# A graph layer with gated mixing and a feed-forward on selected rows: the FFN moved behind the loop, sparse sums on two banks, each tile's row chain one position later

## The chip, the cores and the metric

The kernel runs on one core of one Trainium2 chip. The metric is the device time of one execution in microseconds, median of the runs.

## The reference

`x` is (6250, 256) in float32, with 200,000 edges `src`, `dst`; `dst` is sorted and crowded at its low end.

```python
xn = layernorm(x)
# gnn
h_sparse = keep the 32 largest of each row of xn @ W_neigh
neigh = segment_sum(h_sparse[src], dst) / max(degree, 1)
gnn = xn @ W_self + neigh
# mix: softmax(k) over rows, per-head context, gate
mix = ((q @ (softmax(k, rows)^T v)) * sigmoid(gelu(ln(xn) @ Wg1 + bg1) @ Wg2 + bg2)) @ Wproj + bproj
x2 = x + gnn + mix
# ffn on the k - 1 = 3124 rows with the largest logit w, of 6250
x3 = layernorm(x2); w = x3 @ wr + br
y = (gelu(x3 @ w1 + b1) @ w2 + b2) * w          # w1 256x1024, w2 1024x256
out = x2 + x3 + (y where the row is selected, else 0)
```

## The kernel before, in words

Rows are taken in 50 tiles of T = 125. A first part (to about 407 us) normalises x, makes `h_sparse` as two float16 halves in `rows_d`, and prepares the context and the weights. Then comes the loop this case is about, three hardware loops in all (1, 3 and 1 turns of 10 positions), and behind it the selection.

A position n closes one tile's sum over edges. There are two kinds of tile. Eight **dense** tiles (the ones with most edges; n = 9, 14, 19, 24, 29, 34, 39, 46) are summed as a matrix of counts times all rows: `window` (DVE, L1458 and L1466) writes one-hots of pairs of edge chunks, `count_window` (PE, L1036) multiplies them into counts, ACT copies these out (L842), and `from_rows` (PE, L1107) multiplies the counts with rows that ACT's DMAs bring into `hs` in eight pieces (`load_h`, L515). This is spread over the positions ahead of the dense one (`SHARE`, `SUMMED`): 29 sparse positions have windows, 10 have pieces of `hs` instead, and the last three have neither. The 42 **sparse** tiles are summed by `visit`: POOL gathers 128 rows of 1 KB at a time by indirect DMA (L717), four to a group, into a ring of 8 groups; DVE writes the group's one-hots (L1439, a ring of 8); PE multiplies (L1062, and L1063 for the degree) and frees the slot. SP waits for the landings, tells PE, and refills the index stage.

Beside that each position has the work of its rows. PE: `ffn_down` (L1022) and `ffn_up` (L1014) of older rows, then `mix_hidden`, `project`, `mix_open` (L980 to L1006), all float32, then opens the sum's bank (bank 0 for every sparse tile, bank 1 for dense), turns x3, and visits. DVE: the one-hots, base sums (L1519, L1523), the two FFN rows operations (`ffn_rows`, L1429, L1431), then waits for PE's sum (`s_agg`, L1530), takes it out (L1531 to L1536), and runs the row chain (L1542 to L1573: x2, layer norm by an integer root, x3, logit). ACT: loads of x and of the turned rows, gate functions, the FFN's activation (L802), copies, the store of the FFN's rows. The FFN is computed for all rows of a tile, selected or not; its result goes to `yw_d`, x2 + x3 stays in SBUF (`res_all`).

Behind the loop DVE and PE search the threshold (ten rounds of seven candidates, L1606, L1164), with the FFN of the last three tiles between the rounds, compute a 0/1 mask, and DVE adds `mask * yw` into `res_all` (L1668), stored in ten parts by SP and ACT.

Positions are counted from 0; position n ends with the n-th L1530. A matmul in float32 shows as two records in the trace.

## Time and profile before

| | us |
|---|---|
| median of 3 runs | 2461.32 |
| lowest and highest run | 2454.12, 2475.36 |
| profiled execution, its span | 2470.0 |
| mean granted TensorE clock | 0.811 |

The span is from the first to the last instruction of one profiled execution; the times of the rows below are from its start. In a row of a timeline stand start, length, engine, line, operation, tiles and count, and in brackets the engine's idle time before it and what ended that. A row of a stretch has: from and to, length, then busy us and count for PE, PEld (weight loads), DVE, ACT and POOL, then the granted clock, the DMA engines' share and GB/s.

### The profile page before, as it was taken

The page shows a single profiled execution, that of the slowest core. Times are in us where ns is not written, and L with a number is a line of the kernel's source. Part 1 is how long each engine was busy: PE and PEld are TensorE (multiplying, and loading weights), DVE is VectorE, ACT ScalarE, POOL GpSimd, SP SyncE. Part 2 cuts the span into 40 slices and gives each one's busy share as a digit, 9 for nine tenths or more (in the row PEclk, how much of TensorE's full clock was granted, in tenths as well). Part 3 has the DMA queues.
Part 4 walks back from the last instruction along what each step waited for, and adds up shares of the span by engine and source line. Part 5 has one row for each costly group of instructions (what it writes and reads, how often), then busy time and mean ns, then how long its engine had stood idle before and what let it go on. Part 6 is the DMA issues. An engine that isn't in the chain of part 4 may idle for free. (4 is left out here: it accounts for less than half of the span.)

```text
span 2470.0 us, 40137 instructions
## 1 busy us (share of the span) xinstructions
PE 1713.3 (69%) x8913; PEld 1213.6 (49%) x8914; DVE 1289.5 (52%) x4086; ACT 456.7 (18%) x1009; POOL 1068.1 (43%) x1156
## 2 busy tenths in 40 slices
PE   1985556766556676667677767777767778776873
PEld 0552442444335454445455545545545656555662
DVE  6999536544344235635462653553454553644357
ACT  1542210111011011111121111211111212221220
POOL 1455634555544634553443454344244253444230
PEclk8997667777767877888788888878888888888886
DMA  8221422222223522262236227227127127226337
GB/s 168 68 77 55 124 61 64 71 75 79 85 75 103 153 74 65 76 167 75 66 101 138 59 75 178 57 70 184 50 67 186 49 72 165 68 72 149 90 77 188
DMA packets 173360, 239.30 MB, mean 97 GB/s; under 512 B 34148, under 2 KB 141950, under 8 KB 173214
## 3 DMA queue, kind: packets, MB, share of 16 engines
q0 software_dynamic: 46336, 126.03, 18.7%
q10 hardware_dynamic: 87262, 82.20, 13.1%
q1 hardware_dynamic: 39615, 29.27, 5.1%
q8 instruction: 74, 1.21, 0.2%
q14 instruction: 73, 0.59, 0.1%
HBM read 210.89 MB, written 26.01 MB: 96 GB/s over the span
## 5 line engine op out<-in xcount | busy, mean ns | idle before, releaser
L717 POOL DMA_INDIRECT ring<-rows_d,stage x960 | 948.4, 988 | 1174.9 <-PE bank L1062 812.0
L1062 PE MATMUL bank<-ring,region_v 128*125 x1120 | 399.5, 463 | 115.5 <-issue 108.3
L1036 PE MATMUL bank<-region_k 128*125 x830 | 291.6, 456 | 184.1 <-issue 164.7
L1530 DVE TENSOR_SCALAR col_deg<-bank 125x1 f32<-125x1 f32 x50 | 7.9, 158 | 610.9 <-remote 321.9
L1466 DVE TENSOR_SCALAR region_k<-iota,win_start,region_k 128x500 f16 x830 | 305.1, 407 | 29.7 <-issue 26.4
L1439 DVE SCALAR_TENSOR_TENSOR region_v<-iota,tile_start,dstT 128x500 f16 x280 | 205.6, 739 | 182.7 <-issue 144.4
L1062 PEld LDWEIGHTS bank<-ring,region_v 128*125 x1120 | 171.5, 153 | 246.0 <-issue 185.7
L1022 PE MATMUL bank<-region_v 128*125 128x256 f32 x848 | 243.5, 440 | 68.6 <-issue 68.3
L1014 PE MATMUL bank<-region_v 128*128 128x125 f32 x1664 | 230.8, 295 | 73.4 <-issue 72.8
L1036 PEld LDWEIGHTS bank<-region_k 128*125 x830 | 114.6, 151 | 312.0 <-issue 299.7
L1014 PEld LDWEIGHTS bank<-region_v 128*128 128x128 f32 x1664 | 222.9, 210 | 87.9 <-issue 84.6
L1458 DVE SCALAR_TENSOR_TENSOR region_k<-iota,region_k 128x250 f16 x415 | 173.4, 418 | 168.6 <-issue 130.4
L1022 PEld LDWEIGHTS bank<-region_v 128*125 128x125 f32 x848 | 181.8, 221 | 108.0 <-issue 78.8
L842 ACT ACTIVATE region_k<-bank 125x500 f16<-125x500 f32 (+1 forms) x104 | 60.2, 579 | 927.5 <-remote 483.9
L1063 PE MATMUL bank<-ones,region_v 128*125 128x2 f16 x1120 | 197.0, 176 | 3.4 <-issue 3.4
L1063 PEld LDWEIGHTS bank<-ones,region_v 128*125 x1120 | 176.8, 158 | 6.4 <-issue 4.1
L1107 PE MATMUL bank<-region_k 125*125 125x512 f16 x400 | 114.2, 427 | 71.7 <-DMA region_k<-rows_d 65.1
L802 ACT ACTIVATE region_v<-bank,b 128x125 f32<-128x125 f32 x416 | 112.2, 381 | 86.3 <-PE bank L1014 61.8
L789 ACT ACT_TABLE_LOAD x51 | 65.4, 1283 | 261.6 <-issue 119.3
L1107 PEld LDWEIGHTS bank<-region_k 125*125 125x125 f16 x400 | 56.0, 152 | 107.9 <-DMA region_k<-rows_d 72.4
L802 ACT ACT_TABLE_LOAD x51 | 65.4, 1283 | 183.3 <-PE bank L1022 87.7
L925 PE MATMUL bank<-region_r 128*125 128x512 f32 x200 | 96.6, 606 | 0.0
(283 smaller groups left out, 1958.1 us busy)
## 6 DMA issues: line engine op xcount, KB each, us to landing
region_k<-rows_d ACTq DMA_DIRECT2D x48, 672.0 KB
ring<-rows_d,stage POOLq DMA_INDIRECT x960
region_k<-rows_d ACTq DMA_DIRECT2D x16, 784.0 KB
region_v<-xT_d ACTq DMA_DIRECT2D x53, 125.0 KB
xT_d<-region_r ACTq DMA_DIRECT2D x51, 125.0 KB, 2.1
rows_d<-region_r SPq DMA_DIRECT2D x50, 125.0 KB
region_k<-in_x_dram ACTq DMA_DIRECT2D x50, 125.0 KB
yw_d<-region_v ACTq DMA_DIRECT2D x50, 125.0 KB
```

The source lines that it names most:

```text
L717: pool.indirect_dma_start(out=ring[:, c, :], out_offset=None, in_=rows_d, in_offset=bass.IndirectOffsetOnAxis(ap=stage[:, c:c + 1], axis=0 ...
L802: last = act.activation(hidT[:, n, :], bank[(7, 4)[n // 4]][:, n % 4 * T:(n % 4 + 1) * T], ACT.Gelu_apprx_tanh, bias=b1[:, n:n + 1])
L925: m = pe.matmul(bank[1 + s % 2][0:T, :], xT[:, s % 2, k * T:(k + 1) * T], wkv[:, k, :], start=(k == 0), stop=(k == KC - 1))
L1014: m = pe.matmul(bank[(7, 4)[n // 4]][:, n % 4 * T:(n % 4 + 1) * T], w1[:, k, n * 128:(n + 1) * 128], x3T[:, k, :], start=(k == 0), stop=(k ...
L1022: m = pe.matmul(out, hidT[:, n, :], w2[:, n, :], start=(n == 0), stop=(n == NH - 1), skip_group_check=True)
L1036: m = pe.matmul(out, lo, key, start=False, stop=False, skip_group_check=True)
L1062: m = pe.matmul(total, onehot_s, row_s, start=False, stop=False, skip_group_check=True)
L1063: d = pe.matmul(deg_sum, onehot_s, ones16[:], start=False, stop=False, skip_group_check=True)
L1107: m = pe.matmul(dense_sum, counts16[:, b, :], hs[:, q % 2, (b - first) * 2 * C:(b - first + 1) * 2 * C], start=False, stop=False, skip_gro ...
L1439: dve.scalar_tensor_tensor(out=part(hot_bytes, HOT, SLOT_HOT, hot, 0, SLOT_HOT).bitcast(F16).rearrange("p (a t) -> p a t", a=GC), in0=iota ...
L1458: dve.scalar_tensor_tensor(out=part(pair_bytes, HOT_PAIRS, SLOT_PAIR, slot, 0, KEYS_AT).bitcast(F16) .rearrange("p (a t) -> p a t", a=PAIR ...
L1466: last = dve.tensor_scalar(part(pair_bytes, HOT_PAIRS, SLOT_PAIR, slot, KEYS_AT + u * KEYS * 2, KEYS * 2).bitcast(F16), iota[:, 0:KEYS], p ...
```

## The change

The FFN leaves the loop. Each position now writes x3, x2 + x3 and the logit of its tile to `kept_d` (516 words a row) and x2 + x3 to the output. Behind the loop the rank of every row is computed beside the mask; ranks are turned by one-hots and matmuls into `slots`, the row number of each of 3124 selected rows, 25 tiles of them (`SEL`); POOL gathers these rows from `kept_d`, PE and ACT run the FFN in seven teams of up to four tiles (matmuls 500 columns wide), DVE finishes, and POOL scatters the rows over the output. Sparse sums alternate between banks 0 and 4, and the row chain of a tile runs in the next position, behind that one's one-hots. Names of several semaphores in the first part are merged.

```diff
-        deg_sum = bank[2][0:T, 504:506]
+        deg_sum = bank[7][0:T, 0:2]
         def agg_bank(at):
-            return dense_sum if at.dense else bank[0][0:T, :]
+            return dense_sum if at.dense else bank[(0, 4)[at.s % 2]][0:T, :]
...
@@ gpsimd, behind the gathers
+            pool.wait_ge(s_slots, 1)
+            for g, team in enumerate(TEAMS):
+                for j in team:
+                    pool.indirect_dma_start(
+                        out=row_of(j), out_offset=None, in_=kept_d,
+                        in_offset=bass.IndirectOffsetOnAxis(ap=slots[:, j:j + 1], axis=0)).then_inc(s_kept[g], 16)
+            for j in range(SEL):
+                held = min(T, KEEP - j * T)
+                pool.wait_ge(s_fin, j + 1)
+                pool.indirect_dma_start(
+                    out=out_d, out_offset=bass.IndirectOffsetOnAxis(ap=slots[0:held, j:j + 1], axis=0),
+                    in_=row_of(j)[0:held, C:2 * C], in_offset=None).then_inc(s_out, 16)
@@ scalar
+            def store_row(at):
+                u = at.s % 2
+                act.wait_ge(s_res, at.n + 1)
+                act.dma_start(kept_t[:, bass.ds(at.tile, 1), :], rowbuf[:, u:u + 1, :]).then_inc(s_rowout[u], 16)
+                act.dma_start(out_t[:, bass.ds(at.tile, 1), :], rowbuf[:, u:u + 1, C:2 * C]).then_inc(s_rowout[u], 16)
             def position(at):
...
-                hidden(one)
-                keep_x3T(one)
+                act.wait_ge(s_m3, two)
                 gate_open(n + 1)
...
                 gate_hidden(n + 2)
-                act.wait_ge(s_yw, one)
-                act.dma_start(yw_t[:, bass.ds(n, 1), :], yw[:, s % 2:s % 2 + 1, :]).then_inc(s_ywout[s % 2], 16)
+                before = at.before()
+                if before is not None:
+                    store_row(before)
@@ tensor, position
-                pe.wait_ge(s_yw, here)
                 pe.wait_ge(s_pfree, here)
-                ffn_down(one, y_sum)
                 ends.look_ahead(at_)
-                ffn_up(one)
                 spans.look(at_)
-                pe.wait_ge(s_deg, here)
...
-                pe.wait_ge(s_aggfree, here)
+                last = at_.before()
+                pe.wait_ge(s_aggfree, one if last is None or last.dense else here)
+                pe.wait_ge(s_deg, here)
@@ tensor, behind the loop
+            for t in range(NT):
+                pe.wait_ge(s_hotA, t + 1)
+                m = pe.matmul(bank[3][0:T, 0:2 * SEL], rank_hot[:, t, :], tile_ids[:, t, :], start=(t == 0), stop=(t == NT - 1))
+            m.then_inc(s_ids, 1)
...
+            pe.wait_ge(s_slots, 1)
+            turn_x3(0)
+            ffn_up(0, 0, NH - 2)
+            turn_x3(1)
+            ffn_up(0, NH - 2, NH)
+            for g in range(1, len(TEAMS)):
+                ffn_up(g)
+                if g + 1 < len(TEAMS):
+                    turn_x3(g + 1)
+                ffn_down(g - 1)
+            ffn_down(len(TEAMS) - 1)
@@ vector, position
                 if not at_.dense:
                     gathered()
                 ...
+                before = at_.before()
+                if before is not None:
+                    row_chain(before)
                 ...
                 dve.tensor_tensor(base_p, base_x, p_sum, ALU.add).then_inc(s_pfree, 1)
-                hold(dve, s_ywout[u], (half + 1) * 16)
-                ffn_rows(st, n, y_sum, yw[:, u, :], one)
+                gate_pre(n + 2, u, half + 1, two)
+                mix(two)
                 ...
                 dve.wait_ge(s_agg, one)
                 dve.tensor_scalar(col["deg"][:], deg_sum[:, 0:1], 1.0, None, ALU.max).then_inc(s_deg, 1)
                 ...
                 dve.scalar_tensor_tensor(out=agg_sum, in0=total[:, C:2 * C], scalar=1.0 / LO_SCALE,
                                          in1=junk, op0=ALU.mult, op1=ALU.add).then_inc(s_aggfree, 1)
-                gate_pre(n + 2, u, half + 1, two)
-                mix(two)
-                a = st.mark(dve.scalar_tensor_tensor(out=x2, in0=agg_sum, scalar=col["rdeg"][:, 0:1], in1=base_p,
@@ vector, behind the loop
+            dve.scalar_tensor_tensor(out=tile_hot, in0=iota[0:T, 0:SEL]...to_broadcast([T, NT, SEL]),
+                                     scalar=1000.0, in1=rough...to_broadcast([T, NT, SEL]), op0=ALU.add, op1=ALU.is_equal)
             for t in range(NT):
-                dve.scalar_tensor_tensor(out=res_all[:, t, :], in0=yw_all[:, t, :], scalar=selm[:, t:t + 1],
-                                         in1=res_all[:, t, :], op0=ALU.mult, op1=ALU.add).then_inc(s_fin, 1)
+                dve.tensor_scalar(rank_hot[:, t, :], iota[0:T, 0:T], rank_in[:, t:t + 1], None, ALU.is_equal).then_inc(s_hotA, 1)
...
```

In DVE's position the row chain (now the function `row_chain`) stood behind the sum of the halves and stands now behind the one-hots, for the tile before. The new helpers: `turn_x3(g)` turns a team's x3 tiles (two transposes each), `ffn_up(g)` makes 8 x 2 matmuls of up to 500 columns over four banks that ACT empties with the activation, and `ffn_down(g)` makes 8 matmuls of 256 columns for each tile of the team.

## Rows read from the trace of the kernel before

**Rows 1.** The page, part 1: busy us, share of the span, instructions.
```profile
PE 1713.3 (69%) x8913; PEld 1213.6 (49%) x8914; DVE 1289.5 (52%) x4086; ACT 456.7 (18%) x1009; POOL 1068.1 (43%) x1156
```

**Rows 2.** Groups by line, whole span: busy us, mean ns, idle before by releaser.
```profile
L717 POOL DMA_INDIRECT ring<-rows_d,stage x960 | 948.4, 988 | 1174.9 <-PE bank L1062 812.0 <-issue 267.9 <-remote 91.3
L1062 PE MATMUL bank<-ring,region_v 128*125 x1120 | 399.5, 463 | 115.5 <-issue 108.3 <-DVE region_v L1439 4.8 <-SPq L589 1.1
L1466 DVE TENSOR_SCALAR region_k<-iota,win_start,region_k 128x500 f16 x830 | 305.1, 407 | 29.7 <-issue 26.4 <-remote 2.2 <-PE bank L1036 0.8
L1036 PE MATMUL bank<-region_k 128*125 x830 | 291.6, 456 | 184.1 <-issue 164.7 <-DVE region_k L1466 14.5
...
L1530 DVE TENSOR_SCALAR col_deg<-bank 125x1 f32<-125x1 f32 x50 | 7.9, 158 | 610.9 <-remote 321.9 <-PE bank L1146 158.9 <-issue 130.0
```

**Rows 3.** Stretches of time: busy us of each engine, clock, DMA share, GB/s.
```profile
437.00:2397.00 1960.00, 1416.53 (x7692) 1023.45 (x7692) 925.11 (x2794) 341.96 (x739) 862.72 (x876) 0.82 0.37 96
...
622.00:681.00 59.00, 34.92 (x155) 23.03 (x155) 24.38 (x73) 5.08 (x13) 33.26 (x32) 0.70 0.28 81
...
884.00:901.00 17.00, 17.00 (x126) 14.68 (x125) 7.45 (x30) 7.06 (x14) 3.79 (x4) 0.80 0.38 102
...
1281.00:1324.00 43.00, 32.12 (x170) 22.38 (x169) 12.70 (x38) 7.01 (x15) 21.03 (x22) 0.84 0.90 203
...
1592.00:1637.00 45.00, 31.23 (x162) 22.29 (x161) 24.95 (x74) 8.14 (x17) 20.17 (x21) 0.81 0.26 74
...
692.70:697.00 4.30, 4.04 (x25) 2.33 (x25) 4.30 (x14) 0.00 (x0) 3.39 (x4) 1.00 0.25 69
...
697.00:711.60 14.60, 3.41 (x9) 1.31 (x9) 3.43 (x7) 0.00 (x0) 10.99 (x12) 0.66 0.36 106
```

**Rows 4.** Timeline of POOL in position 5: start, length, idle before.
```profile
692.68 0.95 POOL L717 DMA_INDIRECT ring<-rows_d,stage  x1 [15.71 <-PE bank L1062]
...
711.64 0.95 POOL L717 DMA_INDIRECT ring<-rows_d,stage  x1 [0.30 <-issue]
716.45 0.94 POOL L717 DMA_INDIRECT ring<-rows_d,stage  x1 [3.86 <-PE bank L1062]
```

**Rows 5.** Timeline of DVE in position 4.
```profile
622.45 0.16 DVE L1530 TENSOR_SCALAR col_deg<-bank 125x1 f32<-125x1 f32 x1 [14.29 <-remote]
...
623.88 0.48 DVE L1542 SCALAR_TENSOR_TENSOR region_v<-region_k,col_rdeg 125x256 f32<-125x256 f32 x1
...
630.96 2.39 DVE L1439 SCALAR_TENSOR_TENSOR region_v<-iota,tile_start,dstT 128x500 f16 x3 [1.00 <-DVE w_at L1573]
...
648.15 0.42 DVE L1519 TENSOR_TENSOR region_k<-region_k,region_v 125x256 f32<-125x256 f32 x1
...
649.50 0.35 DVE L1431 TENSOR_SCALAR region_v<-region_v,w_at 125x256 f32<-125x256 f32 x1
681.38 0.16 DVE L1530 TENSOR_SCALAR col_deg<-bank 125x1 f32<-125x1 f32 x1 [31.53 <-remote]
```

**Rows 6.** Timeline of PE: position 4, then the end of the loop and the search.
```profile
632.76 0.89 PE L980 MATMUL bank<-region_v,wg1g 128*64 128x125 f32 x4
...
636.30 0.61 PE L992 MATMUL bank<-hgT,wg 65*128 65x125 f32 x4
...
637.08 0.38 PE L1062 MATMUL bank<-ring,region_v 128*125 x1
...
2397.01 3.70 PE L1022 MATMUL bank<-region_v 128*125 128x256 f32 x16
2400.55 3.73 PE L1014 MATMUL bank<-region_v 128*128 128x125 f32 x32
...
2430.70 2.90 PE L1022 MATMUL bank<-region_v 128*125 128x256 f32 x6
```

**Rows 7.** Timeline of DVE behind the loop.
```profile
2404.21 0.20 DVE L1586 TENSOR_SCALAR_CACHE_REDUCE region_v<-w_all 125x50 f32<-125x50 f32 x1 [0.25 <-DVE w_at L1573]
...
2444.19 19.88 DVE L1668 SCALAR_TENSOR_TENSOR region_r<-region_k,region_v,region_r 125x256 f32<-125x256 f32 x50
```

More of the change, by code:

```diff
@@ L70, in build @@
     BODY = 10
-    assert NT * T == N and NT % BODY == 0 and C == 256
+    SEL = -(-KEEP // T)
+    WIDE = 4
+    RW = 2 * C + 4
+    TEAMS = [range(j, min(j + WIDE, SEL)) for j in range(0, SEL, WIDE)]
+    assert NT * T == N and (SEL - 1) * T < KEEP < SEL * T and NT % BODY == 0 and C == 256
     CHUNK = 128
@@ L220, in build @@
         hit_n = region_v.take([T, 7, NT])
[L221 to L222 removed]
+        masks = region_v.take([T, 2 * NT])
         selm = region_v.take([T, NT])
[L224 to L225 removed]
+        colcum = region_v.take([T, 2 * NT])
+        prefix = region_v.take([T, 2 * NT])
+        rank, rough, rank_tile, rank_in = (region_v.take([T, NT]) for _ in range(4))
+        slots = region_v.take([T, SEL], I32)
         after_search, region_v.at = region_v.at, at
@@ new lines, in ffn_up @@
+            def ffn_up(g, first=0, end=NH):
+                wide = len(TEAMS[g]) * T
+                pe.wait_ge(s_x3T, g + 1)
+                for n in range(first, end):
+                    if g * NH + n >= 4:
+                        pe.wait_ge(s_hid, g * NH + n - 3)
+                    for k in range(KC):
+                        m = pe.matmul(up_bank(n)[:, 0:wide], w1[:, k, n * 128:(n + 1) * 128], x3T[:, g % 2, k, 0:wide],
+                                      start=(k == 0), stop=(k == KC - 1))
+                    m.then_inc(s_up, 1)
@@ new lines, in _, with keep_x3T @@
+            dve.wait_ge(s_ids, 1)
+            a = st.mark(dve.tensor_copy(rank, bank[3][0:T, 0:NT]))
+            st.after(a)
+            dve.scalar_tensor_tensor(out=slots, in0=rank[:, SEL:2 * SEL], scalar=float(T), in1=rank[:, 0:SEL],
+                                     op0=ALU.mult, op1=ALU.add).then_inc(s_slots, 1)
+            def keep_x3T(g):
+                dve.wait_ge(s_tx3, g + 1)
+                wide = len(TEAMS[g]) * T
+                for k in range(KC):
+                    last = dve.tensor_copy(x3T[:, g % 2, k, 0:wide], bank[k][:, 0:wide])
+                last.then_inc(s_x3T, 1)
```

446 lines of the change are left out of this document (233 added, 213 removed).

## The prediction

> **What bounds the kernel now.** I read the page first, then the groups by line, then stretches of time, then the timelines of single positions, and last the end. The page [rows 1] shows no engine near its limit: PE 69 percent, DVE 52, POOL 43. So the kernel is bound by turns of engines. The reader should see in [rows 2] what the turns are: POOL's 960 gathers stand idle 1174.9 us, most of it (812.0) until a visit of PE frees a ring slot, and DVE stands idle 610.9 us (12 us in each of 50 positions) before L1530, until PE has closed a tile's sum. The loop from the first L1530 at 437 to the last at 2397 takes 1960 us [rows 3]. The profiled execution has a span of 2470.0 us and the median of the runs is 2461.3, 9 us less; I sum against 2470 and take 9 off at the end.
>
> One position shows the turns. Position 4 lies between the L1530 at 622.45 and that at 681.38, 58.9 us [rows 5]. PE's first visit starts at 637.08, 14.6 us in [rows 6]: until then PE does the FFN of an older tile and the mix, and DVE the chain of the last row (622.45 to 630.96). The ring is full, POOL waits: in position 5 it has waited 15.71 us when it starts again [rows 4]. From then on it issues 16 gathers in 692.68 to 711.64, one per 1.26 us, so a group of four takes 5.1 us. The reader should then compare two stretches of [rows 3]: in the first 4.3 us of these gathers PE is busy 4.04 and DVE 4.30; in the next 14.6 us PE is busy 3.41 and DVE 3.43, each 0.23 of the time, while POOL runs on. No data is missing there; I take it that long runs of gathers slow whatever PE and DVE issue, until POOL pauses (712.6 to 716.45 [rows 4]). I call these slowed stretches. What causes them the rows don't say. They tie a position to POOL's 32 gathers: 14.6 us without POOL, then about 40 us of gathers, then a few us to close.
>
> **What the change removes and adds in the loop.** (1) PE's FFN of a position goes: 16 records of L1022 in 3.70 us and 32 of L1014 in 3.73 us, 7.4 us at the full clock [rows 6]. What is left ahead of the first visit is the mix, 632.76 to 636.9, 4.1 us [rows 6]. DVE loses the two rows operations, some 0.8 us, ACT the eight activations. (2) The row chain (L1542 to the logits, 623.88 to about 629.95, 6.1 us [rows 5]) now stands behind the next tile's one-hots. So they start after the evacuation (622.45 to 623.5) and a us of loop bookkeeping, the 1.00 idle in [rows 5]: about 2 us after the sum is closed where it is 8.5 now. The two banks let PE start its visits without waiting for that evacuation, except behind a dense tile; the degree's column still has one place, and its wait is over within 0.2 us. (3) The waits that are added: ACT waits for the next mix (done early, it was queued ahead of the visits already) and for the row chain ahead of the two stores; behind it on ACT's queue stands the load of the next x tile, which DVE wants only a whole set of one-hots later. I cost both at nothing; without that cover each would show as a landing of a few us.
>
> DVE's own serial work barely shrinks. For position 4: evacuation 1.0, bookkeeping 1.0, one-hots 17.2 (630.96 to 648.15), chain 6.1, base sums and gate 1.3 (648.15 to 649.50 holds about this much besides the rows operations), mix 0.4 and look-ups 0.4: 27.4 us. PE's is mix 4.1, eight visits at 1.43 (399.5 us over 280) and twelve window pairs at 0.70 (291.6 over 415) [rows 2], at most 24, since slowed ones are in these means. With 32 gathers [rows 3] POOL needs 40 us. If nothing slowed anything the position would take 40 us; if DVE made no headway at all in slowed stretches it would take 27.4 + 33 = 60. DVE's headway there is bounded by 0.23 (one-hots, whose loops have many small steps [rows 3]) and 1; the chain is 21 short instructions without loops, so I take 0.3 for the mixture. Slowed time is 40 less 1.5 starts of 4.5 us, 33: DVE does 10 us there, and the position takes 17.4 + 33 = 50.4, a gain of 8. The stretch 1592 to 1637 [rows 3] holds a later, smaller position of 45.2 us with 20 or 21 gathers: DVE 27.1, slowed 18, DVE does 5.4 in it, so 21.7 + 18 = 39.7, a gain of 5.5. I take 6.5 for the 29 positions that have windows: 190 us.
>
> The ten sparse positions that sum rows from hs or lie beside that: 1281 to 1324 shows position 18, with the DMA share at 0.90 and 203 GB/s [rows 3]. They are bound by transfers, and the change adds some: 258 KB of kept rows and 128 KB of output instead of 125 KB, 0.26 MB or 1.3 us at that rate. PE's lost 7.4 us can help only where the DMAs are not the limit. I take 3 each, between -1.3 and 7.4: 30 us. The eight dense positions take 17.0 us with PE busy all of it [rows 3]; without 7.4 of PE, and DVE's 11 us as the next limit, I take 5 each: 40. The last three: 5 each, 15. The loop gains 190 + 30 + 40 + 15 = 275 us.
>
> **What it adds behind the loop.** Now 72.8 us pass from the last L1530 to the end. After: chain as now, 7.0 (2397.2 to 2404.21). The search up to the selected mask takes 40.0 (2404.21 to 2444.19 [rows 7]); it loses three pairs of rows operations, 2.4, and about 1.0 where PE's FFN parts held a round: 36.6. Ranks: six more DVE operations at 0.25, 1.5; the one-hot of 1250 elements, 1.8 (L1466 has 500 in 0.407 [rows 2], this form is slower). 50 rank one-hots of 125 columns: between 0.08 and 0.41 each, nearest to a quarter of the 500-column row plus its start, 0.18: 9 us, range 4 to 20. Last product, copy and slots 1.2. Four gathers of kept rows and their landing 6.5 (four at 1.26 plus something like 1.5; range 5 to 9). Turn and copy of the first team 3.2. The FFN: a record of 256 columns takes 0.231 (3.70 over 16), one of 125 columns 0.117 (3.73 over 32) [rows 6], so 0.44 for 500. A full team has 32 records up, 14.1 us, and 64 down, 14.8: 28.9 us, and there are 6.25 teams: 181. Turning the other tiles adds 50 pairs of 0.117: 11, of which 2 were counted. So 190. ACT's and DVE's part of it is half of what it was in all and lies beside PE. Behind the last product: sum, scaling, one scatter and its landing, 4. The sum is 7.0 + 36.6 + 1.5 + 1.8 + 9 + 1.2 + 6.5 + 3.2 + 190 + 4 = 261 us, 188 more than the 72.8 now. The fifty final sums (19.88 us [rows 7]) and the last stores are in these 72.8 and go. Setup is unchanged but for a missing 125 KB load.
>
> 2470 - 275 + 188 - 9 = 2374; I say 2375.
>
> **A rule against the change.** The gathers at 692.68 and after stand 1.26 us apart whether DVE is busy (until 697) or nearly idle [rows 3, 4]. The Trainium skill, "DMA: Bandwidth & Descriptors", section SWDGE vs HWDGE vs iDMA, says that GpSimd writes the descriptors of its DMAs into SBUF, and that certain VectorE operations lock it out of that while they run. By that rule DVE's busy time and POOL's would add up, and this change puts more DVE work beside gathers. So far the trace disagrees with it as a large cost; as a rival it is priced below from rows.
>
> **Rivals.**
> A. The turns dissolve: visits start about 5 us after the last sum instead of 14.6 and POOL's run starts as much earlier, and DVE's chain vanishes in time that it now idles (12 us a position [rows 2]). Then 42 sparse positions gain 9.6 each, 403, and the dense 40: 443, so 2470 - 443 + 188 - 9 = 2206. Its far end is POOL never waiting: 960 x 1.26 + 8 x 12 = 1306 for the loop, a gain of 654, 1995 in all. For it: 812 us of POOL's waiting. Against: the slowed stretches and the 203 GB/s of position 18.
> B. DVE becomes the serial bound in the loop. Its 27.4 us stay, its chain moves from a time in which POOL stands still into slowed stretches, and headway there is 0.1. Position 4 then takes 24.1 + 33 = 57.1, a gain of 1.8, the 29 windowed ones 52, the dense 40, the others nothing: 92. The end costs its 188: 2470 - 92 + 188 - 9 = 2557, slower. It decides as soon as the loop gains less than 188, 3.8 us a position. For it: DVE's sum is hardly smaller and PE's crawl at 0.23. Against: DVE's 610.9 us of idle time.
> C. The FFN behind the loop runs at the lower clock (1.2 instead of 2.4 GHz). After the gaps of the search six records of 256 columns take 2.90 us [rows 6], 0.48 each against 0.231. That would add 190: 2565. For it: PE's granted clock is 0.66 to 1.00 in the stretches of [rows 3]. Against: this FFN leaves PE hardly a gap, and 48 records in a row run at the full rate.
> D. The lock-out above: POOL's 862.7 and DVE's 925.1 us of the loop [rows 3], with the 0.30 us between gathers, would not overlap; 1210 + 925 = 2135, 175 more than now, so 2470 + 175 + 188 - 9 = 2824. [rows 4] beside [rows 3] speak against it: at 4.30 of 4.30 us of DVE POOL kept 1.26 us.
> That the change doesn't do what it says is covered by B: the banks alternate, but the freed wait was not the last one.
>
> **How the numbers follow.** Chances: forecast 0.51, A 0.26, B 0.16, C 0.05, D 0.01, rest 0.01. The forecast's own range is 2290 to 2460 (loop gain 190 to 350, end 175 to 215). For 8 in 10 I reach down past A's 2206 to 2140 and up to 2545, just short of B. One per cent, about what a measurement of this kernel tells from no change, is 2437 and 2486. Faster by more: nearly all of A and 0.42 of the forecast, 0.68. Within: 0.08 of the forecast and 0.04 of B and between, 0.12. Slower: 0.20.
>
> **What would show it.** The distance between two L1530-like waits in the windowed positions should fall from 58.9 to about 50 early and from 45 to about 40 later; below 45 and 36 it is A, above 56 and 43 B. The idle time before the first one-hots of a tile should be about a us, and DVE's idle time before closing a sum well under 600 us in all. POOL's wait for PE should fall by about what the loop gains. The end should be 250 to 275 us from the last sum, 28 to 30 us a team. The prediction is wrong if a team takes over 40 us, if POOL's gathers stand more than 1.4 us apart, or if position 18 takes under 30 us.

## The result, and the profile after

The changed kernel takes 2509.45 us in the median of four runs (2499.61 to 2514.48), the kernel before 2466.43 us in four runs beside them (2454.12 to 2475.36). The ratio is 1.0207, 95 percent interval 1.0131 to 1.0283; the two medians lie 43 us apart, 1.7 percent. The change is slower beyond the interval, where 2375 us and faster was forecast; whether by more than 2 percent is open. The runs below were made in five groups, each beside the kernel before, which took 1949, 1951 and 1952 us in three of the groups and 2460 and 2496 us (this last one run) in the other two, with the same code and data; I call these the quick and the slow condition, and the recorded result and the trace that the prediction rests on belong to the slow one. Gains and losses are compared within one condition.

The page of the changed kernel, its span and part 1 (busy us, share, instructions), against [rows 1]:
```profile
span 2497.5 us, 35631 instructions
PE 1546.7 (62%) x7023; PEld 1006.7 (40%) x7024; DVE 1280.0 (51%) x4041; ACT 238.0 (10%) x499; POOL 1129.9 (45%) x1207
```
Its groups by line, against [rows 2] (L729 is the old L717, L1616 the old L1530, L1606 the old L1519, L1015 the first matmul of the mix, old L980):
```profile
L729 POOL DMA_INDIRECT ring<-rows_d,stage x960 | 948.1, 988 | 1018.6 <-PE bank L1074 661.9 <-issue 265.5 <-remote 87.6
...
L1032 PE MATMUL bank<-region_v 128*125 128x256 f32 x200 | 93.0, 609 | 5.6 <-issue 5.6
...
L1015 PE MATMUL bank<-region_v,wg1g 128*64 128x125 f32 x208 | 51.9, 395 | 282.2 <-issue 262.3 <-DVE region_v L1471 8.6 <-remote 8.4
...
L1606 DVE TENSOR_TENSOR region_k<-region_k,region_v 125x256 f32<-125x256 f32 x50 | 21.3, 426 | 50.9 <-DMA region_k<-in_x_dram 32.2 <-issue 11.6 <-DVE region_v L1570 7.1
...
L1616 DVE TENSOR_SCALAR col_deg<-bank 125x1 f32<-125x1 f32 x50 | 7.8, 157 | 469.7 <-remote 216.7 <-issue 135.2 <-PE bank L1153 117.6
```
DVE's wait for the closing of a sum fell from 610.9 to 469.7 us and POOL's wait for PE from 812.0 to 661.9. But a new one stands ahead of the mix: 282.2 us of PE idle, nearly all "issue", where the same line of the kernel before has only 38.4 us. The records of the mix also got longer, as L1032 shows beside the same line of before, L997:
```profile
L997 PE MATMUL bank<-region_v 128*125 128x256 f32 x200 | 64.2, 449 | 0.0
...
L980 PE MATMUL bank<-region_v,wg1g 128*64 128x125 f32 x208 | 37.0, 305 | 38.4 <-issue 37.5 <-DVE region_v L1423 0.9
```
And the stretches, against [rows 3]: the loop from the first to the last closing of a sum, then the FFN behind it:
```profile
432.00:2236.00 1804.00, 1090.87 (x5242) 712.42 (x5242) 896.89 (x2696) 95.88 (x200) 862.51 (x876) 0.72 0.43 111
...
2311.40:2489.60 178.20, 178.07 (x666) 120.32 (x666) 25.70 (x49) 35.45 (x56) 46.69 (x40) 0.98 0.16 43
```
The loop takes 1804 us where it took 1960: a gain of 156, not of 275. The end takes 261.5 us from the last closing, against 72.8. The table sorts the loop by kind of position, from one closing to the next; the late stores are explained below.

| us, slow condition | before | change | forecast gain | gain | change with late stores | gain |
|---|---|---|---|---|---|---|
| windowed (28 of the 29; the first ends where the sum starts) | 1352 | 1259 | 183 | 93 | 1193 | 159 |
| with rows from hs (10) | 398 | 381 | 30 | 16 | 399 | -2 |
| dense (8) | 142 | 117 | 40 | 25 | 89 | 53 |
| last three | 68 | 46 | 15 | 22 | 54 | 14 |
| end, from the last closing | 72.8 | 261.5 | -188 | -188.7 | 260.2 | -187.4 |

Each column comes from one profiled execution. A second one of the kernel before has 1337, 407, 148 and 67 us in the first four rows, so gains of 10 us in a row say little. The profiled run with late stores was also the fastest of its ten, 19 us under their median: for all that stands ahead of the last closing, the medians of the runs give the change a gain of 146 us and the late stores one of 206, where the profiles give 161 and 237.

### The profile page after: what moved, and what is told of

Same layout as the page of the kernel before. It is cut to its first block, busy times and chain, and to the rows that moved or that the text cites. A ratio compares the mean times of both kernels' runs of the same rounds, so it can differ in the third digit from the quotient of the medians.

```text
span 2497.5 us, 35631 instructions
## 1 busy us (share of the span) xinstructions
PE 1546.7 (62%) x7023; PEld 1006.7 (40%) x7024; DVE 1280.0 (51%) x4041; ACT 238.0 (10%) x499; POOL 1129.9 (45%) x1207
## 4 chain that ended last, share of the span: by engine, by line
PE 29%; issue 26%; DVE 15%; DVEq 9%; another core or an unknown queue 9%; DMA 8%; ACTq 2%; SPq 1%; POOL 0%; ACT 0%; POOLq 0%
PE bank L1074 6%; PE bank L1048 6%; DMA region_k<-rows_d 5%; PE bank L1193 3%; PE bank L1207 3%; DVE region_k L1507 2%; PE bank L1117 2%; DVEq L459 2%; PE bank L1032 2%; DVEq L1518 2%; DMA gs_wide<-gs_d 2%; DVE region_r L1381 1%; PE bank L1035 1%; DMA region_k<-in_x_dram 1%
## 5 line engine op out<-in xcount | busy, mean ns | idle before, releaser
L729 POOL DMA_INDIRECT ring<-rows_d,stage x960 | 948.1, 988 | 1018.6 <-PE bank L1074 661.9
L1074 PE MATMUL bank<-ring,region_v 128*125 x1120 | 418.9, 478 | 119.1 <-issue 113.9
L1074 PEld LDWEIGHTS bank<-ring,region_v 128*125 x1120 | 178.1, 159 | 250.7 <-issue 195.8
L1616 DVE TENSOR_SCALAR col_deg<-bank 125x1 f32<-125x1 f32 x50 | 7.8, 157 | 469.7 <-remote 216.7
L1015 PE MATMUL bank<-region_v,wg1g 128*64 128x125 f32 x208 | 51.9, 395 | 282.2 <-issue 262.3
L1075 PEld LDWEIGHTS bank<-ones,region_v 128*125 x1120 | 182.5, 163 | 18.7 <-issue 16.9
L1117 PE MATMUL bank<-region_k 125*125 125x512 f16 x400 | 127.8, 467 | 90.9 <-DMA region_k<-rows_d 76.4
L1015 PEld LDWEIGHTS bank<-region_v,wg1g 128*64 128x64 f32 x208 | 33.7, 201 | 286.4 <-issue 283.1
L1032 PE MATMUL bank<-region_v 128*125 128x256 f32 x200 | 93.0, 609 | 5.6 <-issue 5.6
L1193 PE MATMUL bank<-region_k,region_v 128*128 128x500 f32 (+1 forms) x224 | 88.2, 553 | 1.4 <-DVE region_k L1733 1.4
L1207 PE MATMUL bank<-region_v,region_k 128*125 128x256 f32 x400 | 87.3, 379 | 0.0
L753 POOL DMA_INDIRECT out_dram<-region_r,region_v x24 | 28.6, 1191 | 126.8 <-DVE region_r L1753 123.1
L1035 PE MATMUL bank<-region_v 128*125 128x256 f32 x200 | 79.6, 535 | 7.9 <-issue 7.9
```

The source lines that it names most:

```text
L729: pool.indirect_dma_start(out=ring[:, c, :], out_offset=None, in_=rows_d, in_offset=bass.IndirectOffsetOnAxis(ap=stage[:, c:c + 1], axis=0 ...
L1032: pe.matmul(p_sum, xTc[:, turn, k * T:(k + 1) * T], w_self[:, k, :], start=(k == 0), stop=False)
L1035: m = pe.matmul(p_sum, mixT[:, k, :], wproj[:, k, :], start=False, stop=(k == KC - 1))
L1074: m = pe.matmul(total, onehot_s, row_s, start=False, stop=False, skip_group_check=True)
L1075: d = pe.matmul(deg_sum, onehot_s, ones16[:], start=False, stop=False, skip_group_check=True)
L1117: m = pe.matmul(dense_sum, counts16[:, b, :], hs[:, q % 2, (b - first) * 2 * C:(b - first + 1) * 2 * C], start=False, stop=False, skip_gro ...
```

## The experiments

Theory G, as I had it: long runs of gathers slow what the engines issue, and take back what the change frees. Its rivals change from group to group; each is in the texts on record.

**First group (before: 1948.64 us).** The gathers left out, in both kernels:
```
+  pool.memset(ring[:], 0.0)         # once, at the start
   ...
-  pool.indirect_dma_start(out=ring[:, c, :], ...).then_inc(s_land[block][q], 16)   # four of them
+  pool.sem_inc(s_land[block][q], 16 * GC)
```


> The changed kernel with the 960 gathers of the loop left out (the one-hots, the visits and all else run on a ring filled with zeros; the sums are not the reference's). Theory G (the unbroken runs of gathers slow the sequencers of TensorE and VectorE, 0.7 us an instruction in place of 0.05, and this takes back what the change frees): the loop between the first and the last closing of a sum, 1804 us in the changed kernel, falls to what VectorE needs, 1100 to 1300 us, so the whole to 1800 to 2000 us, and no stretch with 0.7 us instructions is left. Rival W (the loop is held by waits of the engines for each other and for the loads of x and of the rows, whatever the gathers do): the loop stays above 1550 us, the whole above 2250 us.

> The kernel before with the same 960 gathers left out. Theory G: the loop, 1960 us, falls to about 1400 us, the whole to about 1900 us; against the changed kernel without gathers the loop is then 200 to 300 us longer, as my sum had it, which shows that the freed time is real and the gathers take it back. Rival W: the difference of the two loops stays what it is with gathers, about 160 us or less.

Measured: 1912.97 us with the change, 1809.70 without it. The loops are 1285 and 1367 us. So the change is worth 82 us in a loop without gathers, not 200 to 300, and costs 187 behind it; rival W had 160 or less. The first surprise was that the kernel before itself took 1949 us and not 2460. Both are the quick condition, in which little is slowed anyway: the gathers cost the kernel before 139 us, not 500. In the windowed positions behind the tenth it makes no difference whether there are gathers: position 36 takes 30.2 us in the changed kernel without them and 29.9 in the run of it with them below. Something else bounds these.

The network in the loop cut to one eighth, in the kernel before:
```
-  for n in range(first, end):        # ffn_up
+  for n in range(first, first + 1):
-  for n in range(first, end):        # ffn_down
+  for n in range(1):
-  for n in range(NH):                # hidden, on ACT
+  for n in range(1):
   ...
```


> The kernel before with the feed-forward network in the loop cut to one eighth (one of the 8 blocks of w1 and of w2 is multiplied, one of the 8 activations done; the turns, waits and VectorE's steps stay; the output is not the reference's). Theory G: what the 7 eighths cost the loop is a good part of the gain of 156 us, since the sequence 'close the sum, then the network, then the visits' gets shorter by some 4 us in each of 50 positions: 150 to 250 us less, 2220 to 2320 us. Rival V (TensorE's network was hidden beside the gathers and VectorE's one-hots, and what gained in the change is the moved chain and the two banks): less than 60 us, 2400 us or more.

Measured: 1903.44 us, ratio 0.9755 (0.9715 to 0.9794), 45 us less. Position 36 takes 28.2 us, and 28.2 also in the kernel before without gathers, which has its whole network. In the quick condition rival V is right: TensorE's network was nearly hidden.

The row chain back behind the closing of its own sum:
```
-  before = at_.before()
-  if before is not None:
-      row_chain(before)
   ...
   assert st.n == STEPS_B and b == STEPS_B - 1
+  row_chain(at_)
```


> The changed kernel with the row chain back behind the closing of its own sum, ahead of the next one-hots, the two banks and the end kept. Theory G: VectorE starts the next one-hots 5 to 6 us later in each sparse position, but this time lies partly beside slowed gathers: 60 to 200 us more than the changed kernel, 2570 to 2710 us. Rival V: the chain's move is the main gain, so the whole loses 250 us or more (2760 us). A third (C: the moved chain only delays the closing of the sum, since VectorE is the serial bound): no difference within 25 us.

Measured: 2144.94 us, ratio 1.0997 (1.0955 to 1.1038). The next group gives 1.0818 for the changed kernel in the same condition, so moving the chain is worth 36 us of loop (1519.5 against 1483.2), under one us a position. That is less than G's 60 us and more than the 25 of C; for the slow condition the move was not tested.

**Second group (before: 1951.05 us).**

> The changed kernel as it is, beside the kernel before, on the chip that this group of runs gets (the first four of my runs were on a chip where the kernel before takes 1949 us, and there only about 30 instructions of the queues take over 0.55 us in the loop, against over 600 in the trace of before that the prediction rests on). Theory G: where the slow issue is missing, the loop of before is 1500 us and the change frees 120 to 200 us of it while the end costs 188 us: between 1930 and 2010 us where before is 1949; where the slow issue is there, 2500 us again. Rival V (the result does not depend on the slow issue): the ratio is 1.02 in both.

Measured: 2108.65 us, ratio 1.0818 (1.0766 to 1.0869). In the quick condition the change costs 158 us, more than the 61 that I gave at most: the end costs the same 188, and of the loop it takes about 25 (1483 against some 1507, which is 1951 less the 368 ahead of the loop, the 74 behind and 2 around the span, both from traces of this condition). The "issue" idle time ahead of the mix is there too, 246 us of it, without any slowed stretch. That is where the next theory came from.

```
-  bank[(0, 4)[at.s % 2]]   ...   pe.wait_ge(s_aggfree, one if last is None or last.dense else here)
+  bank[0]                  ...   pe.wait_ge(s_aggfree, one)
```


> The changed kernel with all sparse sums in bank 0, so that the first visit waits again until the sum before has been closed. Theory G: each of the about 40 changes between sparse positions gets the closing (2.6 to 3 us of VectorE) and a wait back: 60 to 150 us over the changed kernel. Rival V (TensorE is late anyway by its head of the position, about 6 us of mix, project and open): less than 30 us.

Measured: 2107.82 us, ratio 1.0817 (1.0769 to 1.0864): no difference. In the quick condition the second bank is worth nothing, as rival V had it: PE is late by its own head.

```
-  xin = region_k.take([T, C])       # loaded at the start of its position
+  xin = region_k.take([T, 2, C])    # loaded one position earlier, by turns
```


> The changed kernel with two buffers for x, each tile's x loaded one position earlier. The sum of the waits for x in the changed kernel is 32 us (51 us idle ahead of that line). Theory X (that load is on the path since the row chain went in front of it): 20 to 45 us less than the changed kernel. Rival: the closing of the sum waits for TensorE behind it anyway: within 10 us.

Measured: 2108.30 us, ratio 1.0821 (1.0772 to 1.0871): no difference. Theory X falls: the wait for x, 81.6 us in the trace beside it, stood ahead of another wait that took its place.

```
   pool.indirect_dma_start(...).then_inc(s_land[block][q], 16)
+  pool.memset(pace[:], 0.0).then_inc(s_pace, 1)
+  hold(pool, s_pace, done * (RING * GC) + (c + 1))
```


> The changed kernel with a short fill on GpSimd and a wait for it behind each gather, so that gathers follow each other some 0.3 us later. Theory G: where the slow issue is there, the longer distance lowers it, and the whole gets shorter by 50 us or more; where it is missing, the loop gets longer by at most 100 us, since GpSimd is 1.25 us of 1.9 us a gather there. Rival W (gathers are no matter for the issue): longer by 50 to 300 us in both.

Measured: 2460.48 us, 352 more. The distance of two gathers in a run went from 1.25 to 1.87 us, twice what I meant. Both theories named less; it shows only that GpSimd's pace is close to the bound: 960 x 0.62 is 595 us, and 352 of them showed.

**What the trace said then.** One change of position of the changed kernel, quick condition, the timeline of all engines (start us, length us, engine, line):
```profile
1559.63 0.20 PE L1153 MATMUL bank<-zeros 128*125 128x2 f16 x1
...
1560.66 0.42 DVE L1609 TENSOR_TENSOR region_k<-region_k,bank 125x256 f32<-125x256 f32 x1
...
1561.20 0.40 DVE L1471 SCALAR_TENSOR_TENSOR region_v<-region_v,bank 128x250 f32<-128x250 f32 x1
...
1561.44 0.29 ACTq L850 DMA_DIRECT2D kept_d<-region_v  x1
1561.82 0.31 ACTq L851 DMA_DIRECT2D out_dram<-region_v  x1
1562.23 0.33 ACTq L857 DMA_DIRECT2D region_k<-in_x_dram  x1
...
1562.76 0.46 ACTq L815 DMA_DIRECT2D region_v<-xT_d  x1
1563.39 0.79 ACTq L811 DMA_DIRECT2D gs_wide<-gs_d  x1
...
1568.79 0.16 DVE L1616 TENSOR_SCALAR col_deg<-bank 125x1 f32<-125x1 f32 x1 [7.19 <-issue]
...
1569.30 1.09 PE L1015 MATMUL bank<-region_v,wg1g 128*64 128x125 f32 x4 [9.47 <-issue]
```
The sum is complete at 1559.83, and DVE closes it at 1568.79. In between both engines do nothing that is counted as work. The rows of line 459 (the helper that reads a bound from the tensor `bounds` into a register) in the stretch 1559 to 1569.2, durations as min/median/max in ns:
```profile
L459 DVEq TENSOR_LOAD <-bounds x6: 300/416/2434, 1561.1 to 1568.2; - x6
L459 PEldq TENSOR_LOAD <-bounds x6: 297/304/1927, 1561.2 to 1568.2; - x6
```
Six reads on each engine, with the register work around each 0.75 us at best, and single ones of 1.9 and 2.4 us, while ScalarE issues five transfers in a row, the first two of them the new stores. The kernel before has one store of 125 KB at this place of ScalarE's order; now there are two, of 252 and 125 KB, which wait for the row chain. So the moment moved: 40.9 us (median) ahead of the next closing before, 5.8 us in the recorded trace of the change. In the kernel before PE's reads lay under the network and DVE's under its wait for PE. The same line over the whole span in the recorded traces, first before, then after the change:
```profile
L436 PEldq TENSOR_LOAD <-bounds x182: 20/302/1049, 311.8 to 2345.8; - x182
...
L436 DVEq TENSOR_LOAD <-bounds x182: 3/305/707, 325.3 to 2371.9; - x182
```
```profile
L459 PEldq TENSOR_LOAD <-bounds x182: 4/303/2789, 298.3 to 2202.0; - x182
...
L459 DVEq TENSOR_LOAD <-bounds x182: 4/306/2542, 326.5 to 2218.6; - x182
```
The median is the same, the maximum is not. Counted in the loop, reads over 0.6 us are 9 of 172 on PE and 11 of 171 on DVE before (14 and 1 in a second trace), 51 of 170 and 34 of 171 after; their sum went from 57 and 54 us to 114 and 99. In the quick condition it is 55 and 42 long ones. Of DVE's reads there 76 begin within 3 us behind an issue of ScalarE, and all 42 long ones are among them. So two new theories: L (ScalarE's burst of five makes the reads long) and D (the reads themselves bound the windowed positions).

**Third group (before: 2460.36 us, the slow condition).**

> The kernel before as it is, for its trace on the chips of these runs. Theory G: the time that the recorded trace shows over 1950 us is slow issue: the loop between the first and the last closing of a sum is 1500 to 1510 us in place of 1960 us, with the same instructions, and the windowed positions behind the first ten differ by under 1 us from those of the kernel without gathers. Rival: other work (the gathers, the loads) is what takes longer in the recorded trace.

Measured: 2466.25 us, loop 1959.0 us: the recorded case again. The forecast in this text was for the other condition, so it compares in the wrong place; what it shows is that the slow condition comes back, and the runs of this group can be set against the recorded ones.

```
   act.wait_ge(s_m3, two)
   gate_open(n + 1)
+  before = at.before() and at.before().before()
+  if before is not None:
+      store_row(before)               # the tile of two positions before
   ...
   gate_hidden(n + 2)
-  before = at.before()
-  if before is not None:
-      store_row(before)
   ...
```


> The changed kernel with the two stores of a tile's row moved from the end of ScalarE's position, where they are issued in one burst of five with the loads of x, of the turned x and of the gate's scale, to half a position later, behind the gate's tanh. Theory L (the burst falls on the six register loads by which TensorE and VectorE read their bounds, so that 45 to 55 of 170 on each take 1 to 2.4 us in place of 0.3): the long ones fall to under 15 of 170 and the whole gets 40 to 70 us shorter. Rival M (they are long because both engines now read at the same time): within 15 us, the long ones stay.

Measured: 2441.41 us in ten runs, ratio 0.9932 (0.9895 to 0.9969). Against the 1.0207 of the change that is 68 us less (62 by the distances of the medians; the change itself was not run in this group), and it is faster than the kernel before, by 0.3 to 1.1 percent. The reads of line 459 in its trace:
```profile
L459 PEldq TENSOR_LOAD <-bounds x182: 5/301/710, 297.9 to 2117.6; - x182
...
L459 DVEq TENSOR_LOAD <-bounds x182: 3/304/765, 326.2 to 2141.9; - x182
```
Not one over 1 us is left, 5 and 4 over 0.6. PE and DVE still read at the same time in 90 of 170 cases (101 with the change alone), so rival M falls. The idle time ahead of the mix, and ahead of the sum with x, against the 282.2 and 50.9 above:
```profile
L1016 PE MATMUL bank<-region_v,wg1g 128*64 128x125 f32 x208 | 50.2, 388 | 210.8 <-issue 186.9 <-DVE region_v L1472 22.2 <-DVE region_v L1468 1.7
...
L1607 DVE TENSOR_TENSOR region_k<-region_k,region_v 125x256 f32<-125x256 f32 x50 | 21.4, 427 | 16.8 <-DVE region_v L1571 8.3 <-issue 6.7 <-DMA region_k<-in_x_dram 1.8
```
The loop takes 1735 us, 68 less than with the change alone (1803.6). The sum of the reads in the loop fell from 114 to 52 us on PE and from 99 to 51 on DVE, so short reads can account for most of this. They need not be all of it: the edit also takes the wait for the row chain away from ahead of the three loads, and no run parts the two.

**Which store it is.** The trace also has the packets of the transfers. The store to `kept_d` is the only one on ScalarE's queue with packets of 2064 bytes; the other store and the load of x have 1024. In the recorded trace of the change 85 of the 341 reads in the loop meet a packet of 2064 bytes, and 80 of them take over 0.6 us, among them all 64 over 1 us; of the other 256 reads 5 take over 0.6. In the quick condition it is 95 of 105 and 2 of 236, and 108 reads meet only packets of 1024 bytes, none of which is long. So the long reads go with the store to `kept_d`, not with the one to the output. The packets alone are not enough, though: with late stores 12 reads still meet them in the slow condition and 30 in the quick one, and only 2 and 1 are over 0.6. What else it takes stays open.

The reads spread over the position, in both kernels:
```
   for part_of in here:
       window(d, *part_of)
+  if not at_.dense:
+      (behind the last segment) ends.look_ahead(at_)
+      spans.look(at_.after(1), this segment's share of its windows)
   ...
-  ends.look_ahead(at_); spans.look(at_.after(1))     # ahead of the closing
   (changed kernel only, on PE: both reads from ahead of the mix to behind mix_open)
```


> The changed kernel with VectorE's reads of the next position's bounds spread behind its one-hots, one share behind each segment, in place of all of them ahead of the closing of the sum, and TensorE's behind the matmuls of its head. Theory D (VectorE with its register loads, 0.75 us each and about 170 of them, sets the windowed positions, and these loads can pass beside one-hots that are in the engine): 60 to 130 us shorter. Rival: a load waits for the engine in any case, so its place is no matter: within 15 us.

> The kernel before with VectorE's reads spread in the same way (TensorE's stay where they are, under the network). Theory D: VectorE bounds the windowed positions of the kernel before too, and what hid its loads was at most the 3 to 4 us in which it waits for TensorE at the closing: 0 to 60 us shorter. Rival V (TensorE with the network is the bound, as my sum had it): within 10 us.

Measured: 2482.63 us, ratio 1.0110 (1.0031 to 1.0190), with the change, and 2476.54 us, ratio 1.0050 (1.0002 to 1.0099), without it. The first is about 24 us under the change, less than half of the lower end that D gave. The second is slower by 0 to 1 percent, some 12 us: no gain, just outside D's range (0 to 60 us shorter) and V's (within 10), with an interval that reaches into both, so it does not tell the two apart.

**Fourth group (before: 1951.84 us).**

> The changed kernel with both edits together: the row's stores half a position later, and the reads of bounds spread. Theory L and D together: if the two gains are of one cause (the long loads), the sum is hardly better than the late stores alone, 0.985 to 0.995 of the kernel before where that takes 2460 us; if they are independent, 0.975 to 0.985.

Measured: 2059.74 us, ratio 1.0559 (1.0522 to 1.0597). The forecast was for the other condition; what it compares with here is the next run.

> The changed kernel with the late stores once more. Where the kernel before takes 2460 us, the ratio is 0.993 again; where it takes 1950 us, the long register loads, which the trace of the changed kernel shows there too (55 and 42 of 170), go away as well: 50 to 75 us under the 2109 us of the changed kernel, a ratio of 1.045 to 1.058, since the end still costs 188 us and the loop has less to give.

Measured: 2023.58 us, ratio 1.0372 (1.0335 to 1.0410): 85 us under the change in this condition, more than I said; the loop is 1400 us against 1483, and no read takes over 1 us. With the spread reads on top it is 36 us worse. So the two are not independent: what spreading gained was that some reads left the burst (in the trace of the spread reads alone DVE has 11 over 1 us, PE still 35), and without it it does harm. D is not confirmed as I put it. Nor is L, as far as it blames the burst of five. With late stores 104 of DVE's reads begin within 3 us behind an issue, most of them beside the three loads, and one is long. And with late stores and spread reads 11 reads of both engines take 1.15 to 1.86 us: all of them begin 0.8 to 3.3 us behind the store to `kept_d`, with no load issued in the 6 us before. The stores do it without the loads.

> The changed kernel with gathers of half a row (512 of 1024 bytes for each of the 128 indices, so that other values are summed; the same count of gathers and of descriptors). Theory G1 (the bytes in flight slow the issue and hold the positions with loads of rows): the positions with row loads fall by 40 us or more in sum, and where the issue is slow the whole falls by over 100 us. Rival G2 (the descriptors, written by GpSimd, or GpSimd's own pace do it): less than 30 us.


```
-  out=ring[:, c, :],    in_=rows_d,
+  out=ring[:, c, 0:C],  in_=rows_d.rearrange("n (a c) -> (n a) c", a=2),
```
Measured: 2063.23 us, 45 less than the 2108.65 of the change. By kind of position: with rows from hs 325 us against 357, dense 118 against 130, windowed 957 against 959. The bytes of the gathers matter where rows are loaded too or stand beside that (44 us in both kinds, so G1 holds for its first half), and nowhere else; its second half, on slow issue, was not met in this condition.

**The slow condition itself.**

> The kernel before with the gathers left out, once more. Theory G (runs of gathers are what slows the issue where it is slow): where the kernel before takes 2460 us, this one has nearly no queue instruction of 0.55 us or more in its loop and takes 1810 to 1850 us, as where before takes 1949 us. Rival H (the slow issue has another source): the loop stays over 1650 us, the whole over 2150 us. Where before takes 1950 us it only repeats 1810 us.

The edit is that of the first group. Measured: 1814.80 us, with before at 1952: only a repeat of 1810. The last group met the slow condition (before: 2496.34 us, one run).

> The kernel before with the gathers left out, in hope of the condition in which the kernel before takes 2460 us. Theory G (the runs of gathers are what slows the issue there): 1810 to 1850 us, as where before takes 1949 us. Rival H (another source): over 2150 us. Where before takes 1950 us it only repeats 1810 us and the question stays open.

Measured: 1812.59 us. Where the kernel before takes 2496, the same kernel without gathers takes what it takes in the quick condition. The line that carries DVE's loop over window pairs shows it best, first in the recorded trace of before, then in this run (its L1474):
```profile
L1477 DVEq MOVE  x492: 2/36/725, 382.7 to 2230.2; - x164
L1477 DVEq ALU_OP  x388: 3/40/723, 383.3 to 2233.0; - x194
```
```profile
L1474 DVEq MOVE  x492: 36/36/36, 331.5 to 1620.6; - x164
L1474 DVEq ALU_OP  x388: 40/40/47, 332.1 to 1621.2; - x194
```
Theory G is right in this: in the slow condition the gathers are what slows the issue, up to 0.72 us for an instruction of 0.04, and without gathers nothing of it is left. Of some 8400 register and branch instructions of PE and DVE in the loop 458 take over 0.55 us in the recorded trace of before and 474 in that of the change; in the quick condition there is none. What makes the condition stays open. The record numbers the chip 8 in the first group (1949 us) and in the third (2460 us), so this number does not decide it. The distance from gather to gather in a run is the same in both (medians 1.254 and 1.251 us).

> The kernel before with the network in the loop cut to one eighth, once more. Where the kernel before takes 1950 us it took 1903 us. Theory G in the condition of 2460 us: there the network's 150 instructions a position are issued ahead of the visits in slowed stretches, so that it costs more than the 41 us of the other condition: 100 to 200 us less than before. Rival: the network is hidden there too, and the 224 us that the change frees with late stores come from the moved chain: less than 60 us.

Measured: 2362.65 us, 134 less than the one run beside it and 98 less than the 2460 of the third group; the loop is 1852.6 us against 1959.0. So seven eighths of the network in the loop cost some 106 us in the slow condition and some 43 in the quick one. Of the whole G named 100 to 200 us: 134 lies inside, 98 just under it, and both are clear of the rival's 60.

## Why the prediction was wrong, step by step

**The end was right in its sum, in part by luck.** 188 us more were forecast, 188.7 came. From the last closing to the first matmul of the FFN it is 75.5 us, where the sum had 66.8 (the four gathers of kept rows and their landing alone take 10.3, not 6.5); the FFN takes 178, where it had 190; behind it are 7.9, where it had 4. The errors cancel. PE is busy 178.07 of 178.20 us there, at a granted clock of 0.98: rival C did not happen.

**The step that failed** is item (3) of the part on the loop: "The waits that are added: ACT waits for the next mix [...] and for the row chain ahead of the two stores [...] I cost both at nothing". The stores were looked at as something that stands ahead of the load of x. That cover held in the quick condition: two buffers for x changed nothing. What I did not count is what the stores do to others. They fall on the moment at which PE and DVE read their bounds, and the reads became long. Moving the two stores, with their wait, by half a position is worth 68 us in the slow condition (ratio 1.0207 to 0.9932) and 85 us in the quick one. The packets point at the store to `kept_d`; by what path it holds up a read no run tells.

**The second term that was mis-sized** is "look-ups 0.4" in DVE's serial work of a position. In the position shown above they run from 1561.0 to 1568.7; with short reads six of them are about 4.5 us. Before, they lay under a wait that the change takes away, and on PE under the network. So removing the network laid its reads bare: 38 us of idle time ahead of the mix became 282, and 211 with the late stores. The reads are not all that it covered: the kernel before with one eighth of the network has 179 us there in the slow condition, and 156 of them end with DVE's L1423. That PE's 7.4 us a position would go was right as work and wrong as time: seven eighths of them are worth 106 us of loop in the slow condition, 2 a position.

**A third term, "the mix, 4.1 us", was too small as well.** It stands ahead of the first visit, and I took its records at the rate of the kernel before. In the loop the five lines of the mix keep PE busy 209 us before, 285 with the change, which is 5.7 us a position, and 277 with late stores; the granted clock of the loop fell from 0.82 to 0.72, and the kernel before with one eighth of the network has 258. How much of this time reached the loop's length no run shows. Of the 119 us that the loop gained too little (156 for 275) the late stores give back 68; the other 51 stay open, and this term is the nearest candidate.

**The 6.5 us of a windowed position** came out as 3.3, and as 5.7 with the late stores; my 0.3 for DVE's headway in slowed stretches was not tested by itself. The ten positions with rows from hs gave 16 of 30 us, and nothing with the late stores, both near what two traces of one kernel differ by (9). I had named the transfers and still taken 3 each; half the bytes a gather gives 33 us there (in the quick condition), where the change adds bytes. The dense ones gave 25 of 40, with the late stores 53.

**The rivals.** B was right in its number's direction: it decides "as soon as the loop gains less than 188", and the loop gained 156. Its mechanism (DVE's headway of 0.1) is not what the late stores show: with them the loop gains 224 and the kernel is faster than before by 0.7 percent. A did not happen, and D did not: POOL keeps 1.25 us (median) in both kernels. Where DVE is idle all through a gather, the next one follows after 1.25 us in the mean; where DVE is busy for nine tenths of it or more (some 95 gathers in either kernel), after 1.38 and 1.39. All that the gathers in runs take over 1.25 us sums to 40 us before and 39 after, where D had 175 more. The Trainium skill, "DMA: Bandwidth & Descriptors", section SWDGE vs HWDGE vs iDMA, says that VectorE, in one of its modes, locks GpSimd out of the SBUF state into which it writes descriptors. The traces agree with it in direction; that busy times would add up, as D had it, they do not show.

**The signs I named.** The first one-hots of position 4 start 1.4 us after the closing (603.72 and 605.14): right. DVE's wait for the sums fell to 470 us: it should have been well under 600, and was; but 244 us of new idle time came ahead of PE's mix, so this sign alone said little. The windowed positions are to be read in two parts. Positions 1 to 6 went from 58.6 to 51.2 us in the mean, near the forecast 50; the other 22 went from 45.5 to 43.3 instead of 40, on B's side of the border. With late stores it is 49.6 and 40.7, where the forecast had them. A single position tells little: position 4 alone fell to 36.7, and to 47.6 with late stores. Of the three things that would prove the prediction wrong none came (a team takes 28.1 us, gathers stand 1.25 us apart, position 18 takes 46.1, against 39.1 before), and it was wrong all the same: none of them looked at the waits that I had put at nothing.

**The condition.** The forecast holds for the slow condition alone, as does any reading of the slowed stretches. In the quick one the change is 8.2 percent slower, and 3.7 with the late stores; the end costs the same there and the loop gained some 25 us, 107 with late stores. A version that beats both kernels was found in the slow condition only, by 0.7 percent: the change with late stores.

## What to carry to other kernels

Before work is taken out from between two engines, look at what it covers in the queues: register reads and DMA issues are not counted as busy, so the cover shows only as an "issue" wait that is missing. For each DMA that a change moves, look not only at what it delays behind it, but at what the other engines' queues do while its packets run. Work that is moved out of a loop into an end without cover costs its full time there; what it gives back in the loop is the part that was on the path, here 2 us of 7 a position.

## What the runs showed of the hardware

A read of a register from an SBUF tensor (TENSOR_LOAD) takes 0.30 us in the median in every trace here, and up to 2.8 us in the recorded trace of the change while the packets of a store of 125 rows of 2064 bytes run, which ScalarE has just issued; without gathers it is as long (2.9 us at most in the changed kernel without them), and with late stores 0.8 at most. Behind the one store of 125 KB of the kernel before, 5 of the 66 reads of PE that begin within 5 us take over 0.6, at most 1.05. Indirect gathers go with slow queues of other engines in one condition and not in another: instructions of 0.04 us take up to 0.72, the same kernel takes 1950 or 2460 us, and without gathers 1810 and 1813. And TensorE's granted clock in the loop fell from 0.82 [rows 3] to 0.72 with the network out of it, so it was at the lower of its two levels (1.2 and 2.4 GHz) for more of the time; no run separates what that costs.
